# Peaks of W on ScalarE, later POOL adds, and a lagged low part of W in the first tile of a two-stage layer

## The reference, cut to what matters

```python
x1 = x + matmul(fake_quant(layernorm(x)), fake_quant(ctx))   # x: (2, 512, 1024), ctx: (2, 1024, 1024)
y = layernorm(x1)
logits = y @ W_router.T                                      # 8 experts, top 2, softmax weights "combine"
h = einsum('nd,erd->ner', y, A_stack) * combine[..., None]   # 8 experts of rank 16
out = x1 + y @ W_base.T + b_base + 2 * einsum('ner,eor->no', h, B_stack)
```

## Time and profile before

| | before |
|---|---|
| time, median of 3 runs | 185.98 us (185.98 to 186.04) |
| profiled execution, its own time | 187.33 us |
| its span, first to last instruction | 185.5 us |
| TensorE busy | 166.9 us (90%) |
| VectorE busy | 119.7 us (65%) |
| ScalarE busy | 73.6 us (40%) |
| POOL busy | 61.2 us (33%) |
| mean granted TensorE clock | 0.972 |

### The profile page before, as it was taken

One profiled execution on the slowest core, in us unless ns is written; L12 is line 12 of the kernel. 1 busy time (PEld: TensorE's weight loads), 2 busy tenths in 40 slices (PEclk: granted clock), 3 DMA queues, 4 the chain that ended last, 5 costly groups with the idle time before them and its releaser, 6 DMA issues.

```text
span 185.5 us, 2626 instructions
## 1 busy us (share of the span) xinstructions
PE 166.9 (90%) x964; PEld 89.8 (48%) x964; DVE 119.7 (65%) x276; ACT 73.6 (40%) x98; POOL 61.2 (33%) x141
## 2 busy tenths in 40 slices
PE   6879889899974896894999999999999999999992
PEld 3444334455631344461556556556556556556541
DVE  7894579999989947774824934833843842822821
ACT  3096357999849902315222222223123123120000
POOL 8804776888840000056180072062040040000000
PEclk9999999999999589998799999999999999999999
DMA  5999999999400000000200200300200200200211
GB/s 116 398 419 410 410 408 408 410 410 409 178 0 2 0 0 4 0 0 0 113 0 5 113 0 0 117 0 0 113 4 0 113 0 0 114 3 0 112 59 57
DMA packets 6780, 22.74 MB, mean 123 GB/s; under 512 B 880, under 2 KB 1136, under 8 KB 6768
## 3 DMA queue, kind: packets, MB, share of 16 engines
q1 hardware_dynamic: 6624, 22.58, 31.2%
q10 hardware_dynamic: 144, 0.00, 0.0%
HBM read 18.38 MB, written 4.19 MB: 122 GB/s over the span
## 4 chain that ended last, share of the span: by engine, by line
PE 62%; DVE 27%; issue 5%; POOL 3%; ACT 0%; DVEq 0%; POOLq 0%
PE ps L812 44%; PE ps L802 5%; PE ps L772 4%; DVE xs L520 3%; PE ps L781 3%; DVE bnx L451 2%; DVE w_lo L591 2%; DVE bnx L449 2%; DVE a_t L513 2%; PE ps L795 2%; PE ps L793 2%; PE ps L794 2%; DVE diag L538 2%; DVE xs L529 2%; POOL root L248 1%
## 5 line engine op out<-in xcount | busy, mean ns | idle before, releaser
L812 PE MATMUL ps<-w_hi,yt_hi 128*128 128x512 f16 x128 | 41.2, 394 | 5.0 <-DVE w_lo L591 5.0
L812 PE MATMUL ps<-w_hi,yt_lo 128*128 128x512 f16 x128 | 40.8, 391 | 0.0
L812 PE MATMUL ps<-w_lo,yt_hi 128*128 128x512 f16 x128 | 40.8, 391 | 0.0
L772 PE MATMUL ps<-a,a_t 128*128 128x512 f16 x128 | 31.2, 379 | 1.8 <-DVE a_t L513 1.0
L247 POOL TENSOR_SCALAR root<-mvy 128x1 f32<-128x1 f32 (+1 forms) x7 | 1.5, 218 | 72.3 <-DVE mvy L445 72.2
L619 DVE MAX8 top<-ps 128x8 f32<-128x8 f32 x8 | 1.4, 174 | 37.1 <-PE ps L795 37.1
L318 ACT ACTIVATE a<-stage,prm,inv_s 128x1024 uint8<-128x1024 f32 x16 | 19.4, 1240 | 10.3 <-DMA stage<-in_ctx_kv 10.2
L812 PEld LDWEIGHTS ps<-w_hi,yt_lo 128*128 128x128 f16 x128 | 12.8, 100 | 16.0 <-issue 1.6
L812 PEld LDWEIGHTS ps<-w_lo,yt_hi 128*128 128x128 f16 x128 | 12.9, 101 | 15.9 <-issue 2.1
L812 PEld LDWEIGHTS ps<-w_hi,yt_hi 128*128 128x128 f16 x128 | 11.9, 101 | 17.6 <-issue 6.0
L772 PEld LDWEIGHTS ps<-a,a_t 128*128 128x128 f16 x128 | 11.9, 98 | 15.7 <-DVE a_t L513 2.5
(11 more groups left out here) (134 smaller groups left out, 273.8 us busy)
## 6 DMA issues: line engine op xcount, KB each, us to landing
stage<-in_ctx_kv SPq DMA_DIRECT2D x16, 512.0 KB, 13.5
stage<-in_w_t SPq DMA_DIRECT2D x8, 512.0 KB, 10.7
xs<-in_x SPq DMA_DIRECT2D x7, 512.0 KB, 13.8
out_dram<-xs SPq DMA_DIRECT2D x7, 512.0 KB, 2.7
ar_raw<-in_ar_t SPq DMA_DIRECT2D x1, 544.0 KB, 15.5
xs<-in_x SPq DMA_DIRECT2D x2, 256.0 KB, 3.7
b_raw<-in_b_t SPq DMA_DIRECT2D x1, 512.0 KB, 11.2
bias_sb<-in_bias SPq DMA_DIRECT2D x1, 512.0 KB, 12.0
```

Source lines behind the costliest of these rows:

```text
L772: last = nc.tensor.matmul(ps[:, s1_bank(t) + h, :], a1_t[:, t % 4, k, :], a2[:, n, h * H:(h + 1) * H], start=k == 0, stop=k == K - 1)
L812: ins = nc.tensor.matmul(ps[:, OUT_BANK[p] + h, :], part, rhs[:, k, h * H:(h + 1) * H], start=k == 0 and part is hi and rhs is w_hi, stop= ...
```

## The change

The peak of the last W tile moves from VectorE to ScalarE, whose split of `ar` now comes ahead of `make_y(0)`. The correction of tile 2 moves from POOL to VectorE, and POOL's next add (tile 3) waits for the split of b; POOL's wait for the last `w_lo` is gone. VectorE's queue is reordered: W's peaks come ahead of `take_a1t(7)`, `split_ar` goes up to just behind `scale_w`, `sum_x1(7)` goes down behind `split_w(3)`, and `split_hct(0)` comes ahead of `split_b`. On ScalarE `split_b` goes up ahead of `split_w(3)`, and `gate_weight(t)` ahead of `make_y(t + 1)`. On TensorE the peak product of W moves to the start of tile 7 and `transpose_y(0)` into tile 7; six extra products keep it busy before tile 0; in tile 0 the low-part products run three steps behind the others; `transpose_y(1)` and `transpose_hc(0)` come earlier by steps, and `transpose_y(2)` later.

```diff
-        PEAKS = 2 + K - 1
+        PEAKS = 2 + K
         FIRST = 2
+        FIRST_ADDS = 3
+        LAG = 3
...
-            return (x1_ready_first, t + 1) if t < FIRST else (x1_ready, t + 1 - FIRST)
+            return (x1_ready_first, t + 1) if t < FIRST_ADDS else (x1_ready, t + 1 - FIRST_ADDS)
...
             scale_y(0, 2)
-            add_corr(2)
+            pool.wait_ge(b_lo_ready, 1)
             add_corr(3)
             scale_y(2, 3)
-            pool.wait_ge(w_lo_ready, K)
             add_corr(4)
...
             make_corr(1)
-            for k in range(4, 7):
+            for k in range(4, K):
                 peak_w(k)
+            split_ar()
             make_y(0)
-            split_ar()
+            split_w(0)
             split_first_yt()
-            split_w(0)
             split_w(1)
             split_w(2)
             make_y(1)
+            split_b()
             for k in range(3, K):
                 split_w(k)
-            split_b()
             gate_weight(0)
...
             for t in range(1, T):
+                gate_weight(t)
                 if t + 1 < T:
                     make_y(t + 1)
-                gate_weight(t)
-                if t + 1 < T:
                     sum_row(t + 1)
...
             scale_ar()
+            add_corr(2)
             sum_x1(5)
-            peak_w(7)
+            peaks_w()
             take_a1t(7)
-            peaks_w()
             scale_w()
+            split_ar()
             sum_x1(6)
+            split_w(0)
             split_first_yt()
-            split_w(0)
-            sum_x1(7)
             split_w(1)
             split_w(2)
-            split_ar()
             split_w(3)
-            split_w(4)
+            sum_x1(7)
             dve.wait_ge(iota_ready, 1)
             nc.vector.tensor_copy(expert[:, :], expert_i[:, :]).then_inc(expert_ready, 1)
+            split_w(4)
             split_w(5)
             dve.wait_ge(expert_ready, 1)
             gate_tile(0)
             split_w(6)
             split_w(7)
+            split_hct(0)
             split_b()
-            split_hct(0)
             split_yt(1)
...
+            def wide_high(k):
+                for part, rhs in ((yt_hi, w_hi), (yt_lo, w_hi)):
+                    for h in range(NH):
+                        nc.tensor.matmul(ps[:, OUT_BANK[0] + h, :], part[:, 0, k, :], rhs[:, k, h * H:(h + 1) * H],
+                                         start=k == 0 and part is yt_hi, stop=False)
+
+            def wide_low(k):
+                pe.wait_ge(w_lo_ready, k + 1)
+                for h in range(NH):
+                    nc.tensor.matmul(ps[:, OUT_BANK[0] + h, :], yt_hi[:, 0, k, :], w_lo[:, k, h * H:(h + 1) * H],
+                                     start=False, stop=False)
...
-                    if t == T - 1 and k == 2:
+                    if t == T - 1 and k == 0:
                         pe.wait_ge(w_diag_ready, 1)
...
-                    if t == T - 2 and k == 7:
+                    if t == T - 1 and k == 3:
                         pe.wait_ge(ar_scale_ready, 1)
                         transpose_y(0)
...
+            keep_busy(6, 5)
             pe.wait_ge(x1_summed, T - 1)
             pe.wait_ge(first_half_lo, 1)
             for k in range(K):
                 if k == K // 2:
                     pe.wait_ge(yt_lo_ready, 1)
-                pe.wait_ge(w_lo_ready, k + 1)
-                wide(0, k, False)
-                if k == 4:
+                pe.wait_ge(w_hi_ready, k + 1)
+                wide_high(k)
+                if k >= LAG:
+                    wide_low(k - LAG)
+                if k == 3:
                     pe.wait_ge(x1_summed, T)
                     pe.wait_ge(yt_lo_ready, 1)
                     pe.wait_ge(ar_lo_ready, 2)
                     narrow(0)
+                if k == 3:
+                    transpose_y(1)
                 if k == 5:
-                    transpose_y(1)
-                if k == 7:
                     transpose_hc(0)
+            for k in range(K - LAG, K):
+                wide_low(k)
...
-                    if k == 3:
+                    if k == (5 if t == 1 else 3):
                         transpose_y(t + 1)
```

More of the change, by code:

```diff
@@ L153, in xattn_ffn @@
         x_scaled, x_measured, x_quantised = (sem(n) for n in ("x_scaled", "x_measured", "x_quantised"))
-        x_quantised_pool, x1_ready_first, w_peak_vec = sem("x_quantised_pool"), sem("x1_ready_first"), sem("w_peak_vec")
+        x_quantised_pool, x1_ready_first = sem("x_quantised_pool"), sem("x1_ready_first")
         a1_transposed, a1t_ready = sem("a1_transposed"), sem("a1t_ready")
@@ L530, in add_corr @@
                                         ALU.add).then_inc(x1_ready_first, 1)
[L532 to L535, removed]
             def spread(peaks, i):
@@ L575, in peaks_w @@
                 dve.wait_ge(peaks_act, PEAKS)
-                dve.wait_ge(w_peak_vec, 1)
                 then(nc.vector.tensor_reduce(top_w[:, :], peak[:, 2:2 + K], AX.X, ALU.max))
@@ L819, in _, with keep_busy @@
                 nc.tensor.matmul(ps[:, COLSUM_BANK, 0:3 * P], ones16[:, 0:P], ones16[:, :], start=True, stop=True)
-            def keep_busy(count):
+            def keep_busy(count, bank):
                 for _ in range(count):
-                    nc.tensor.matmul(ps[:, 0, 0:3 * P], ones16[:, 0:P], ones16[:, :], start=True, stop=True)
+                    nc.tensor.matmul(ps[:, bank, 0:3 * P], ones16[:, 0:P], ones16[:, :], start=True, stop=True)
             column_sums(0, 0)
-            keep_busy(6)
+            keep_busy(6, 0)
             column_sums(0, 1)
-            keep_busy(4)
+            keep_busy(4, 0)
             pe.wait_ge(ident16_ready, 1)
```

## The result

The changed kernel takes 176.84 us (median of 4 runs, 176.83 to 176.85) against 185.98 us before: a ratio of 0.9511, 95% interval 0.9494 to 0.9527. The forecast was 175.6 us in a range of 174.6 to 178.4.

The account below looks back on a forecast made before the run. TensorE, 90% busy, was held by waits for W's low part, `hc` and W's peaks, plus a halved clock, between 51 and 88 us. Gains 6.0 + 4.35 = 10.35 us off 185.98 gave 175.6 us, range 174.6 to 178.4.

Parts of the forecast that it names:

- the eighth peak: W tile 7's peak on ScalarE: runs 47.9 to 49.1, VectorE asks at 50.1, so it costs nothing, 1.0 us of cover.
- the spread: VectorE's spread of W's peaks, 2.25 us while POOL adds: claimed to take 0.24 us with POOL empty.
- the scale: Scale of W on VectorE, after the peak product: claimed ready at 52.7, 2.0 us earlier.
- POOL's last steps: Last small steps of `scale_y(0, 2)` beside VectorE's `add_corr(2)`: may be held 1.1 us, `y_bias` at 49.5 instead of 48.4.
- C: Rival: the spread stays long because POOL is not its cause, `w_diag` 2.0 us later; 177.6 us, chance 0.04.
- D: Rival: hand-overs with 0.6 us of cover or less come late, TensorE waits 0.5 to 1.5 us; 176.6 us, chance 0.13.
- E: Rival: clock falls at tile 0's start and stays low until tile 1, 12.15 us lost; 187.8 us, chance 0.02.
- the last line of the sum: From span to median: profiled span 175.15, execution 177.0, then median 185.98 - 10.35 = 175.6 us.
- the whole 10.35 us: Total gain claimed: 6.0 us up to `narrow(1)` plus 4.35 us in tile 1.
- the 4.35 us of tile 1: Gain claimed in tile 1, which takes 14.16 us without its `hc` wait: `narrow(2)` at 87.6 instead of 97.97.
- forecast A: Main case, every step as worked out: 174.8 to 176.2 us, chance 0.64.
- Rival B: Clock falls inside tile 0 of the changed kernel, losing 1.75 to 3.4 us; say 178.2 us, chance 0.14.

## Why the prediction was right, point by point

*Schedule.* Nearly every step came as worked out: the eighth peak hidden; the spread at 0.25 us; the scale ready at 52.7, 2.0 us earlier; POOL's last steps held for 0.9 us (1.1 forecast); 0.2 us (0.3 forecast) before `split_w(3)`; 1.05 us (1.2 forecast) before `narrow(0)`; `hc` of tiles 0 and 1 in time; `narrow(1)` 0.16 us and `narrow(2)` 0.12 us ahead of the forecast; the later tiles at their rate. Rivals C, D and E did not come; the tightest of D's seams, `hc` of tile 0, was met within 0.1 us, and C is refuted twice, by the spread beside POOL's add and without it.

*The step that was mis-sized* is the last line of the sum, from span to median. I took the whole 10.35 us off the median, 185.98, because it lay 1.35 under the profiled execution. Between the two profiled executions 10.5 us went (185.5 - 175.0), but only 7.6 of them are schedule; the other 2.9 were two falls of the clock in the one before (185.5 against 182.6). In the sum they hide in VectorE's idle time before the first gate, 3.51 us where an execution without a fall has 1.88, and in the 4.35 us of tile 1, where such an execution has 2.95 to gain. The median execution loses only 1.6 us to the clock, so it could give back only 7.6 + 1.6 = 9.2; measured were 9.14. The sound way was there in the same paragraph: 175.15 + 1.83 = 177.0, measured 176.84. That the time fell in the range is luck in part: 176.84 lies above forecast A (174.8 to 176.2) and in the band of rival D, whose late hand-overs did not come.

*The clock.* Rival B named the right mechanism and the right size for a short fall (1.7 us) but not its place: it is in the kernel before, in most executions, and in the experiments that leave or make a gap of over 2 us. Its price for a long one, 3.4 us, is too high where waits cover a part: the 6.8 us at the low level in tile 0 of the kernel before put off `narrow(1)` by 1.56 us. The changed kernel, whose gaps there are at most 1.05 us, had a clock of 1.00 in all four runs, and a gap of 1.6 us brought no loss. By the Trainium skill, TensorE: Matmul & The Clock Gate, "The HAM clock gate", the lower level follows an idle stretch; the trace agrees that gaps bring the fall, but it can come after work has begun again, as in the earlier trace rows.

*What the parts are worth*, at the full clock and at `narrow(1)` where in tile 0: POOL's adds 1.3 us (shown from both sides), the earlier `narrow(0)` 2.0 (shown in the kernel before), the exponential 3.0 there and a wait of 2.57 in the changed kernel. The remaining 1.3 of 7.6 us would be the 0.94 before `hct_lo` and the earlier peak product; this split was not tried by itself. VectorE's queue gives the same total: 2.0 us from the scale, 1.88 before the gate and 0.94 before `hct_lo`, less the new 0.18, are 4.6 us up to `narrow(1)`, and 3.0 in tile 1 make 7.6. The lag is worth -0.24 and the six products nothing.

## What to carry to other kernels

Carry a gain over from span to span, and add what lies outside; before trusting the distance of one profiled execution from the median, read the span and clock of several, since one with a fall of the clock counts as schedule what is luck. Where one engine's queue runs without idle up to a seam, a tenth of a us of idle in it is a tenth of the time, and a small operation stuck behind a neighbour (an exponential, a spread, a copy of eight elements) can cost more than the large ones. A description of a change is a hypothesis too: two of its parts, the lag and the filling, could be left out at no loss.

## What the runs showed of the hardware

VectorE's spread (`tensor_scalar`, 16-bit, from and to SBUF) and its copy of 8 elements don't run beside POOL's add of two SBUF tiles: 2.25 and 1.50 us for 0.25, 1.41 for 0.17, each ending within 0.06 us of the add. I had expected it of the spread, not of the copy. The Trainium skill, SBUF — State Buffer, "Who interferes with whom", allows for both: copies, casts and `tensor_scalar` can take the port pair that VectorE shares with GpSimd. Not every one does here: the `tensor_scalar` of one column took 0.21 us beside the same add as the copy. `split_yt(1)` with one input from PSUM took 1.22 us beside such an add in the changed kernel (71.43 beside 71.59), its usual time.

A loss to the clock comes in steps of 1.4 to 1.7 us here (184.4 to 186.0; 186.0 to 187.4; 178.1 to 179.8), and whether it comes differs from run to run of the same program: of the kernel before, 13 executions in 58 had none. With `narrow(0)` earlier all five had one, which is too few to say that it became more frequent. A mean clock under 1 need not cost time: with the exponential first, two executions with 0.989 took 181.45 and 181.51 us beside 181.39 with 1.0.
